# Attention in steps of two images: the relative step ahead of the weighing of an older pair, and the stores of queries and keys spread

## What is computed

```python
# 16 images of 14 x 14 positions, 192 channels, 12 heads of 16
q, k, v = heads(x @ qkv_w + qkv_b)
rel_h = einsum('bhwc,hkc->bhwk', q as rows and columns, Rh)
rel_w = einsum('bhwc,wkc->bhwk', q as rows and columns, Rw)
attn = softmax(scale * q @ k.T + rel_h[..., :, None] + rel_w[..., None, :])
out = (attn @ v) @ proj_w + proj_b
```

## Time and profile before

| | us |
|---|---|
| median of 3 runs (1831.34 to 1839.41) | 1836.53 |
| the profiled execution | 1837.3 |
| its span | 1834.8 |
| PE busy | 1470.4 (80%) |
| DVE busy | 1112.0 (61%) |
| ACT busy | 763.6 (42%) |
| POOL busy | 429.3 (23%) |
| mean granted clock of TensorE | 0.767 of full |

### The profile page before, as it was taken

The page is one execution under the profiler, slowest core; times in us unless marked ns, Lnnn a source line. Parts: engine busy times, 40 slices in busy tenths (PEclk is TensorE's granted clock), DMA queues, the critical chain, the costliest instruction groups (busy, mean ns, idle before and its releaser), DMA issues. The chain is left out here.

```text
span 1834.8 us, 49543 instructions
## 1 busy us (share of the span) xinstructions
PE 1470.4 (80%) x19315; PEld 1248.7 (68%) x19315; DVE 1112.0 (61%) x3772; ACT 763.6 (42%) x1702; POOL 429.3 (23%) x686
## 2 busy tenths in 40 slices
PE   4768888888875967767977999899988786877887
PEld 4767777777764846656765667688875675665766
DVE  7877777777787435444656674544436643534554
ACT  3633333333345523333434333555552652433442
POOL 2712222222252100000032210556650310000004
PEclk9955555555567978888986569999995796978998
DMA  3000000000013683546615303422334565544932
GB/s 86 1 20 4 4 4 4 4 4 4 4 40 96 157 241 98 150 108 137 126 42 165 107 14 143 138 79 90 92 92 144 163 151 198 143 117 103 182 73 59
DMA packets 71586, 164.46 MB, mean 90 GB/s; under 512 B 17698, under 2 KB 42730, under 8 KB 68860
## 3 DMA queue, kind: packets, MB, share of 16 engines
q1 hardware_dynamic: 65980, 148.44, 31.0%
q0 software_dynamic: 5376, 12.85, 2.3%
HBM read 93.84 MB, written 67.42 MB: 88 GB/s over the span
## 5 line engine op out<-in xcount | busy, mean ns | idle before, releaser
L1279 ACT ACTIVATE l_arena<-l_ps 98x784 f32<-98x784 f32 x192 | 158.4, 825 | 321.8 <-PE l_ps L1137 319.9
L514 PE MATMUL gru_ps_r<-gru_hp,gru_wp 128*128 128x16 f16 x3920 | 199.9, 176 | 67.9 <-DVE gru_hp L489 67.9
L1337 DVE TENSOR_REDUCE l_mt<-l_ps 98x4 fp32r<-98x784 f32 x192 | 187.1, 974 | 87.3 <-PE l_ps L1116 85.3
L514 PEld LDWEIGHTS gru_ps_r<-gru_hp,gru_wp 128*128 128x128 f16 x3920 | 150.6, 106 | 88.3 <-DVE gru_hp L489 88.3
L1116 PE MATMUL l_ps<-l_arena,l_arena 128*98 128x196 f32 x768 | 122.1, 287 | 89.0 <-DVE l_mt L1337 86.3
L514 PE MATMUL gru_ps_n<-gru_hp,gru_wp 128*128 128x16 f16 x3920 | 191.2, 174 | 0.0
L1306 DVE TENSOR_TENSOR l_arena<-l_ps,l_arena 56x448 fp32r<-56x448 f32 x84 | 64.7, 772 | 207.7 <-ACT l_arena L1244 207.5
L1116 PEld LDWEIGHTS l_ps<-l_arena,l_arena 128*98 128x98 f32 x768 | 98.0, 190 | 103.5 <-DVE l_mt L1337 84.4
L514 PEld LDWEIGHTS gru_ps_n<-gru_hp,gru_wp 128*128 128x128 f16 x3920 | 150.0, 104 | 0.0
L580 ACT ACTIVATE gru_reset<-gru_ps_r,gru_unscale 128x32 f32<-128x32 f32 x196 | 56.3, 287 | 216.2 <-PE gru_ps_r L514 216.2
L1041 POOL CAST l_rec_parts<-l_sums 98x32 fp32r<-98x32 f32 x24 | 5.0, 210 | 563.8 <-DVE l_sums L1316 563.8
(11 more groups left out here) (378 smaller groups left out, 4072.0 us busy)
## 6 DMA issues: line engine op xcount, KB each, us to landing
l_arena<-qk SPq DMA_DIRECT2D x96, 294.0 KB
qk<-l_arena SPq DMA_DIRECT2D x48, 392.0 KB, 6.1
rel<-l_arena SPq DMA_DIRECT2D x24, 686.0 KB
l_arena<-rel SPq DMA_DIRECT2D x48, 343.0 KB
qk<-l_arena SPq DMA_DIRECT2D x12, 784.0 KB, 11.5
l_arena<-in_experts_dram SPq DMA_DIRECT2D x8, 1152.0 KB, 7.6
l_arena<-x SPq DMA_DIRECT2D x24, 294.0 KB, 6.5
l_arena<-x SPq DMA_DIRECT2D x24, 196.0 KB, 3.0
```

Of the source, the lines that this page charges most:

```text
L514: last = pe.matmul(out[:, b, B * m:B * m + B], wp[:, wi, g, m, :], hp[:, b, part, B * k:B * k + B], start=False, stop=True, skip_group_che ...
L1279: act.activation(probs[g % SLOTS][:TH, :, :], banks, ACT.Exp).then_inc(p_ready, 1)
L1337: dve.tensor_reduce(mt[:TH, i % 2, :], ps[:TH, S_BANK:S_BANK + 2, :TB].rearrange("p c (h k) -> p c h k", h=2), AXIS.X, ALU.max, negate=Tru ...
```

## The change

The loop goes in 48 steps of two images on all engines (`STEPS`), and the number of steps between an image's exponential and its weighing is `LAG` = 2. On TensorE a step is: logits by query of the even image, a relative step, the weighing of the pair two steps older, logits by query of the odd image, logits by key of both, and in three of the steps a second relative step. On ScalarE the relative copy and the copy of the older pair come first, then both exponentials; on VectorE maxima of the even image, relative subtraction, copy, maxima of the odd image. The fourteen relative steps of a set take the first eleven steps of its 32 images: `REL_FIRST` and `REL_SECOND`. ScalarE waits for stored relative sums only once, before the third set's first. On SP the second set's ten stores of queries and keys move from the front of the loop into turns 9 to 18, the third set's into every third turn from 23 to 50; the relative stores are at turns 8 and 22 of a set; storing the reciprocals is one turn later, after the load of the next sums. The reciprocal is after the maxima of a step's odd image. GpSimd's loop over the same reciprocals is written in one piece.

```diff
-    LAG = 4
+    STEPS, LAG = IMAGES // 2, 2
     REL = 14
-    REL_STEPS = (1, 2, 3, 4, 5, 6, 7, 8, 10, 12, 14, 16, 18, 20)
+    REL_FIRST = (0, 2, 4, 6, 7, 8, 9, 10, 11, 12, 13)
+    REL_SECOND = (1, 3, 5)
...
-                    if i % 5 == 3 and i < 50:
-                        store_qk(2, i // 25, [i // 5 % 5])
-                    if i - 1 in rel_of_step and rel_of_step[i - 1] % 7 == 6:
-                        quad, j = divmod(rel_of_step[i - 1], REL)
-                        store_rel(quad, j // 7)
+                    if 9 <= i < 19:
+                        store_qk(1, (i - 9) // 5, [(i - 9) % 5])
+                    if 23 <= i < 53 and i % 3 == 2:
+                        store_qk(2, (i - 23) // 15, [(i - 23) // 3 % 5])
+                    quad, at = divmod(i, 2 * B)
+                    if quad < QUADS - 1 and at in (8, 22):
+                        store_rel(quad + 1, at // 22)
...
-                    if i >= 21 and i % 8 == 5:
-                        store_reciprocals((i - 21) // 8)
+                    if i >= 22 and i % 8 == 6:
+                        store_reciprocals((i - 22) // 8)
...
-                for half in range(2):
-                    store_qk(1, half)
-                for i in range(IMAGES + LAG + 1):
+                for i in range(IMAGES + 2 * LAG + 1):
                     main_step(i)
...
-                for i in range(IMAGES + LAG):
-                    if i < IMAGES:
-                        logits_by_query(i)
-                    if i in rel_of_step:
-                        rel(rel_of_step[i])
-                    if i > LAG and (i - LAG) % 2 == 1:
-                        weigh_values(i - LAG - 1)
-                    if 1 <= i <= IMAGES:
-                        logits_by_key(i - 1)
+                for n in range(STEPS + LAG):
+                    if n < STEPS:
+                        logits_by_query(2 * n)
+                    if n in rel_first:
+                        rel(rel_first[n])
+                    if n >= LAG:
+                        weigh_values(n - LAG)
+                    if n < STEPS:
+                        logits_by_query(2 * n + 1)
+                        logits_by_key(2 * n)
+                        logits_by_key(2 * n + 1)
+                    if n in rel_second:
+                        rel(rel_second[n])
...
-                    if r >= REL and r % 7 == 0 and r > REL:
-                        act.wait_ge(rel_stored, 32 * (r // 7))
+                    if r == 2 * REL:
+                        act.wait_ge(rel_stored, 128)
...
+                for n in range(STEPS + LAG):
+                    if n in rel_first:
+                        rel(rel_first[n])
+                    if n >= LAG:
+                        keep_even(n - LAG)
+                    if n < STEPS:
+                        exponentials(2 * n)
+                        exponentials(2 * n + 1)
+                    if n in rel_second:
+                        rel(rel_second[n])
...
+                for n in range(STEPS + LAG):
+                    if n < STEPS:
+                        maxima(2 * n)
+                    if n - 1 in rel_second:
+                        rel(rel_second[n - 1])
+                    if n in rel_first:
+                        rel(rel_first[n])
+                    if n >= LAG:
+                        keep_odd(n - LAG)
+                    if n < STEPS:
+                        maxima(2 * n + 1)
+                    if n >= 9 and n % 4 == 1:
+                        reciprocals((n - 9) // 4)
```

More of the change, by code:

```diff
@@ L852, in kept_rows @@
             return o_quad[p // 2][row:row + 64, b * T:(b + 1) * T]
-        rel_of_step = {2 * B * quad + at: REL * (quad + 1) + j for quad in range(QUADS - 1) for j, at in enumerate(REL_STEPS)}
+        rel_first, rel_second = ({B * quad + at: REL * (quad + 1) + j for quad in range(QUADS - 1) for at, j in enumerate(order)}
+                                 for order in (REL_FIRST, REL_SECOND))
         def first_order(rel, item):
@@ L1048, in _ @@
                 pool.memset(v_flat[:TH, 2 * B * VW:], 0.0).then_inc(ones_ready, 1)
[L1049 to L1052, removed]
+                for h in range(2 * PAIRS):
                     split_reciprocals(h)
@@ L1139, in logits_by_key, with weigh_values @@
                     last.then_inc(t_summed, 1)
[L1141 to L1146, removed]
+                def weigh_values(pair):
+                    p, b = divmod(2 * pair, B)
+                    pe.wait_ge(p_ready, 2 * pair + 2)
+                    if pair >= 1:
+                        pe.wait_ge(even_kept, pair)
+                        pe.wait_ge(odd_kept, pair)
                     for keys in range(2):
@@ L1152, in weigh_values @@
                                 last = pe.matmul(ps[row:row + 32, O_BANK, :T], v_flat[:TH, place:place + 32],
-                                                 probs[(g + odd) % SLOTS][:TH, head, keys * T:keys * T + T],
+                                                 probs[(2 * pair + odd) % SLOTS][:TH, head, keys * T:keys * T + T],
                                                  start=keys == 0, stop=keys == 1, skip_group_check=True)
@@ L1265, in _, with keep_even, exponentials @@
                 last_order(item, value)
-                def keep_even(g):
-                    act.wait_ge(o_summed, g // 2 + 1)
-                    if g == 2 * B:
+                def keep_even(pair):
+                    act.wait_ge(o_summed, pair + 1)
+                    if pair == B:
                         act.wait_ge(qk_stored[1], 160)
[L1270 to L1277, removed]
-                        banks = ps[:TH, T_BANK + 2 * (g % 2):T_BANK + 2 * (g % 2) + 2, :TB]
-                        act.activation(probs[g % SLOTS][:TH, :, :], banks, ACT.Exp).then_inc(p_ready, 1)
-                    if i > LAG and (i - LAG) % 2 == 1:
-                        keep_even(i - LAG - 1)
-                    if i in rel_of_step:
-                        rel(rel_of_step[i])
+                    act.activation(kept_rows(2 * pair), ps[:64, O_BANK, :T], ACT.Copy).then_inc(even_kept, 1)
+                def exponentials(g):
+                    act.wait_ge(t_summed, g + 1)
+                    if g >= SLOTS:
+                        act.wait_ge(o_summed, (g - SLOTS) // 2 + 1)
+                    banks = ps[:TH, T_BANK + 2 * (g % 2):T_BANK + 2 * (g % 2) + 2, :TB]
+                    act.activation(probs[g % SLOTS][:TH, :, :], banks, ACT.Exp).then_inc(p_ready, 1)
+                for n in range(STEPS + LAG):
[8 more added lines that the diff above has]
+                        rel(rel_second[n])
                 for n in range(NT):
@@ L1306, in rel, with keep_odd, maxima @@
                     dve.tensor_tensor(rel_out(r, 64), rel_sums(r), rel_out(r, 0).bitcast(f32), ALU.subtract).then_inc(rel_low, 1)
-                def keep_odd(g):
-                    dve.wait_ge(o_summed, g // 2 + 1)
-                    if g == 2 * B + 1:
+                def keep_odd(pair):
+                    dve.wait_ge(o_summed, pair + 1)
+                    if pair == B:
                         dve.wait_ge(qk_stored[1], 160)
-                    dve.tensor_copy(kept_rows(g), ps[64:128, O_BANK, :T]).then_inc(odd_kept, 1)
+                    dve.tensor_copy(kept_rows(2 * pair + 1), ps[64:128, O_BANK, :T]).then_inc(odd_kept, 1)
+                def maxima(g):
+                    dve.wait_ge(s_summed, g + 1)
+                    if g >= 2:
+                        dve.wait_ge(t_summed, g - 1)
+                    dve.tensor_reduce(mt[:TH, g % 2, :], ps[:TH, S_BANK:S_BANK + 2, :TB].rearrange("p c (h k) -> p c h k", h=2),
+                                      AXIS.X, ALU.max, negate=True).then_inc(max_ready, 1)
                 def reciprocals(h):
@@ L1349, in divide @@
                     if n == 0:
-                        dve.wait_ge(even_kept, IMAGES // 2)
-                        dve.wait_ge(odd_kept, IMAGES // 2)
+                        dve.wait_ge(even_kept, STEPS)
+                        dve.wait_ge(odd_kept, STEPS)
                     if n >= 2:
```

17 lines of the change are left out of this document (2 added, 15 removed).

## The result

The changed kernel takes **1729.78 us** (median of 4 runs, 1728.82 to 1733.38) against 1835.16 us (4 runs, 1831.34 to 1839.41): ratio 0.943, 95% interval 0.940 to 0.946. The profiled execution took 1728.82 us, its span is 1726.2 us, 108.6 us less than the one before.

What follows compares the result with a forecast made beforehand. The prediction took a chain of engine hand-overs, with the exponential inside the loop of the one relative-sums bank, as the bound. Profiled 1837.3 us, less 92.0 from the two layers, plus 3.6 for the ends, gave 1749 us; range 1732 to 1785.

Steps and rivals of the forecast that it cites:

- the charge for the lower clock in the height steps: Attention loops: half of each stretch's four height steps at the lower clock, 2 x 2.1 = 4.2 us per 32 images.
- the ends: Before and after each attention loop: exponential table load 1.3 us, late last reciprocal 0.5 a layer; together 3.6 us added.
- the time outside the loops: All code outside the two attention loops: no term of its own, carried over unchanged within the profiled 1837.3 us.
- width steps: Two-image steps with a relative over widths: VectorE's chain takes 5.5 us against 6.29, no clock loss.
- Height steps: Steps with height relatives: 6.8 us for a double, 6.1 for a single, some 25.5 for four at full clock.
- Plain steps: Two-image steps without a relative: taken at 3.7 us, no gain, with 3.6 to 3.8 for the range.
- Waits: ScalarE's two 5.2 us waits a layer for stored relatives go; VectorE's waits for sums, 9.8 us, too; inside the 92.0.
- Stores: Query and key stores of the second set moved into the loop, the third's spread: cost taken as 0.
- transfers: Rival: same bytes in 232 instead of 277 us, reciprocals wait for sums, 26 us come back: 1775 us; chance 0.14.
- No effect of the reorder: Rival: VectorE's wait ahead of odd maxima keeps steps long, only waits go: about 1807 us; chance 0.04.
- The reciprocals: Slower rival: reciprocals in VectorE's row between two pairs' maxima wait for SP's loads, costing 123 us: 1872 us; chance 0.04.
- The clock stays low: Rival: all steps with a relative run at 1.2 GHz, a layer takes 262 us: 1811 us; chance 0.10.

Runs made afterwards that it cites:

- the stores put back: Changed kernel with the second and third sets' query and key stores where they were before: 1730.0 us, ratio 0.942.
- the transfers alone: Kernel before, its order of work kept, with the changed kernel's SyncE list and ScalarE's single wait for stored relatives: 1808.1 us, ratio 0.984.

## Why the prediction was right and where it was wrong

Right were the direction, the mechanism and most terms; the sum was 20.2 us too high for the profiled execution (1749 against 1728.8), and the range's low end 2.2 us too high for the median. Three terms failed: the charge for the lower clock in the height steps (16.8 us taken, some 6.5 measured), the ends (3.6 taken, nothing seen), and the time outside the loops, which was put at no change without a reason and shrank by 8.6. The width steps, 4.9 us too short in the forecast, hid a part of that by luck. Exponentials 0, 64 and 95 of the first layer in the timeline after, to set beside the earlier trace rows:

```profile
644.50 0.82 ACT L1280 ACTIVATE l_arena<-l_ps 98x784 f32<-98x784 f32 x1
...
815.62 0.83 ACT L1280 ACTIVATE l_arena<-l_ps 98x784 f32<-98x784 f32 x1 [1.25 <-PE l_ps L1136]
...
872.40 0.82 ACT L1280 ACTIVATE l_arena<-l_ps 98x784 f32<-98x784 f32 x1
```

And 0 and 95 of the second layer:

```profile
1446.70 0.82 ACT L1280 ACTIVATE l_arena<-l_ps 98x784 f32<-98x784 f32 x1
...
1672.85 0.82 ACT L1280 ACTIVATE l_arena<-l_ps 98x784 f32<-98x784 f32 x1
```

The layers take 227.9 and 226.2 us, 231.0 was forecast: 8.0 us of the 20.2. The ends' 3.6 are the next; the last 8.6 lie outside the loops (108.6 less the 51.2 and 48.7 that the loops gave).

- **Width steps**: 5.65 against 5.5. The chain was right to 0.06 us up to logits by key; its last piece, by key and by query, measured 1.02 and was counted 0.36 + 0.56. Over 28 steps this was 4.9 us too little in the forecast, with two steps of 5.95 us at a clock of 0.71 among them; the other 26 had 1.00. The copy cut up, the copy last and the weighing ahead each moved the step by their own length, so this chain is shown.
- **Height steps**: the term mis-sized most. The forecast had 25.5 us for four of them and 4.2 for the clock, 29.7; measured were 26.0, 28.9, 26.1 and 26.5 in the four stretches, 11.3 us less in all. The four of the second set, first layer, as windows cut at the even maxima (length, engines, PEclk):

```profile
641.95:646.63 4.68, 4.06 (x36) 3.45 (x34) 2.57 (x4) 3.74 (x5) 0.00 (x0) 1.00 0.95 184
646.63:653.67 7.04, 5.32 (x36) 5.14 (x36) 3.19 (x5) 2.62 (x5) 0.00 (x0) 0.76 0.55 103
653.67:661.69 8.02, 6.30 (x52) 4.97 (x52) 3.55 (x6) 2.92 (x6) 0.00 (x0) 0.79 0.58 116
661.69:667.99 6.30, 4.38 (x48) 3.58 (x49) 3.55 (x6) 2.25 (x5) 0.00 (x0) 1.00 0.28 70
```

  At 1.00 a double height step was seen at 6.98 to 7.03 us, a single one at 6.30, so 6.8 and 6.1 were each 0.2 low; the first step, which has nothing ahead of it, takes 4.68 or 5.15 and was too dear at 5.8 (25.5 less two times 6.8 and 6.1). Four such steps come to 25.0 or 25.5 us, so the sum at the full clock held, and the charge for the clock did not. The lower clock is there, in two of these four steps, as taken; but the step at 0.79 cost 1.0 us, and the one at 0.76 nothing to be seen (it has no weighing yet, 36 matmuls against 52, and no run shows it at 1.00), while 2.1 was taken for each. Only in the third set of this layer was it worse: its single step took 8.64 us at 0.60. By stretch the clock cost some 1.0, 3.4, 1.1 and 1.0 us, where 4.2 was taken each time.
- **Plain steps**: 3.72 against 3.7. From exponential 64 to 95 the last stretch is 56.8 us in both layers, and the 57.6 of the earlier trace rows was taken over: the other 1.6 of the 8.0 us.
- **Waits**: ScalarE's for stored relatives are gone; VectorE's for sums are 5.8 us in both layers, below the 10 named.
- **Stores**: nothing, as the stores put back show.
- **Ends**: wrong. The 1.3 us a layer for the exponential's table were not paid:

```profile
642.65 0.54 ACT L1247 ACTIVATE l_arena<-l_ps 56x448 fp32r<-56x448 f32 x1 [2.06 <-PE l_ps L1102]
643.21 1.28 ACT L1280 ACT_TABLE_LOAD   x1
...
645.54 0.83 ACT L1280 ACTIVATE l_arena<-l_ps 98x784 f32<-98x784 f32 x1 [0.21 <-PE l_ps L1136]
```

  The load ends at 644.49 and delays the first exponential at most; but exponentials are off the chain now, by the same change, and VectorE went on with the odd maxima at 643.87. From the second layer's last maxima to the end of the span it is 1726.2 - 1671.17 = 55.0 us, and it was 1834.8 - 1779.73 = 55.1 before.
- **Outside the loops**: the step that was missing. Of its 8.6 us 2.6 lie ahead of the first exponential, and 6.1 are the dense part between the layers, here as a window in the trace before:

```profile
1068.80:1181.00 112.20, 106.81 (x497) 78.85 (x496) 65.52 (x92) 51.02 (x74) 30.83 (x26) 0.92 0.29 99
```

After:

```profile
1012.90:1119.00 106.10, 103.19 (x497) 76.56 (x496) 65.74 (x92) 51.01 (x74) 30.35 (x26) 0.96 0.30 104
```

In the kernel with subtraction and copy behind both maxima:

```profile
1002.40:1114.50 112.10, 106.71 (x496) 78.87 (x496) 65.55 (x92) 51.05 (x74) 30.73 (x26) 0.92 0.29 99
```

  The same 500 or so matmuls take 106 or 112 us, at a mean granted clock of 0.96 or 0.92, and most other kernels had 110.3. What decides which it takes stays open. The forecast took one profiled execution of 1837.3 us as if all but the loops stood still. The span less the two loops, from first to last exponential, was 1280.8 us in that execution, the longest of all 14 kernels traced (1270.2 at the shortest), and 1272.2 after. The range had no term for this; a few us for it would have held the result.

The rivals: *transfers* fell, with a DMA share of up to 1.00 and 5.8 us waited for them. *No effect of the reorder* fell, its 1807 us being what the transfers alone gave. *The reciprocals* are the 5.8. *The clock stays low* fell for this order, and the kernel with the exponential in the loop shows that it was a real one: there it was 0.72 with widths. The Trainium skill, page TensorE: Matmul & The Clock Gate, section on PSUM-queue depth-cycling, describes such a loss in a kernel that cycles through PSUM banks. The trace of the kernel with the exponential in the loop shows a loss beside one bank passed round (0.72); the changed kernel, which passes the same bank round and has 1.00 with widths, shows none there, so the one bank does not decide by itself.

What stays open: why the clock falls in one or two of four height steps and not always in the same ones. No run was made for it alone; in the two kernels with the weighing in the wait for the bank it stayed at 1.00 from the third step on.

## What to carry to other kernels

Write the chain of a step down from one timeline, with the handing engine of each link, and see what stands in it that need not: an exponential there cost 201 us, a 0.36 us copy 16. An instruction belongs where its engine waits for another: the same weighing lengthened a width step, whose relative matmuls were late, from 5.65 to 6.55 us, and shortened a height step, whose relative matmuls waited for their bank, from 6.96 to 5.99. When a loop gets out of a chain, ask again of each small fixed cost (a table load) whether it is still on it, and give the range a term for the code that does not change, since one profiled execution can lie at the edge of what that code takes.

## What the runs showed of the hardware

The copy of 196 columns out of PSUM took 0.365 us on VectorE in one instruction and 0.585 in four (56.2 us for 96), 0.327 and 0.495 on ScalarE (47.5 us for 96): three more instructions cost 0.22 and 0.17 us. They overlap: 384 of 0.209 us would be 80 us end to end and were 56.2. On VectorE 0.4 to 0.6 had been expected. And the same step can differ by its clock: the one of 6.96 us at 1.00 took 8.27 at 0.79.
